# FP4 input groups quantised, scaled and turned in two halves, with the second three slots later, and two slots' exponentials moved up

## What is computed

```python
x = L0_attn_x                                  # (2, 2048, 128)
h = _layernorm(x) * (1 + ca) + sa
x = x + ga * attention(h, Wq, Wk, Wv)          # RoPE, causal up to one key beyond
h = _layernorm(x) * (1 + cb) + sb
x = x + gb * ffn(h)                            # all three products in FP4
...
def fp4_quant_dequant(x):
    xb = x.reshape(shape[:-1] + (shape[-1] // 16, 16))
    scale = jnp.maximum(jnp.max(jnp.abs(xb), axis=-1, keepdims=True) / 6.0, 1e-12)
    xn = xb / scale
    idx = jnp.searchsorted(_MID, jnp.abs(xn))
    return (_GRID[idx] * jnp.sign(xn) * scale).reshape(shape)
def ffn(x):                                    # w_gate, w_up: (352, 128)
    return fp4_linear(silu(fp4_linear(x, w_gate)) * fp4_linear(x, w_up), w_down)
```

## Time and profile before

| what | value |
|---|---|
| median of 3 runs | 661.08 us (659.02 to 661.5) |
| the profiled execution's own time | 660.58 us |
| its span, from first to last instruction | 658.8 us |
| busy: PE, DVE, ACT, POOL | 609.0, 464.8, 355.0, 246.5 us |
| mean granted TensorE clock | 0.994 |

### The profile page before, as it was taken

The page is one execution under the profiler, slowest core; times in us unless marked ns, Lnnn a source line. Parts: engine busy times, 40 slices in busy tenths (PEclk is TensorE's granted clock), DMA queues, the critical chain, the costliest instruction groups (busy, mean ns, idle before and its releaser), DMA issues.

```text
span 658.8 us, 10990 instructions
## 1 busy us (share of the span) xinstructions
PE 609.0 (92%) x3763; PEld 477.3 (72%) x3763; DVE 464.8 (71%) x1265; ACT 355.0 (54%) x740; POOL 246.5 (37%) x305
## 2 busy tenths in 40 slices
PE   7998899989799899999989998888999999999997
PEld 5665777868576777785668787666677888777775
DVE  3887689786787447826668978679756673777765
ACT  4334554665545464453445456555656556666554
POOL 4275655453764321003556545467452100000000
PEclk9998999999899999999999999999999999999999
DMA  8300000000000000000000000020000000000101
GB/s 250 108 1 1 1 1 1 1 0 1 1 1 0 1 1 1 1 1 1 0 1 1 1 1 1 0 61 2 1 1 0 1 1 1 1 1 16 36 29 48
DMA packets 12494, 9.65 MB, mean 15 GB/s; under 512 B 1868, under 2 KB 10904, under 8 KB 12440
## 3 DMA queue, kind: packets, MB, share of 16 engines
q1 hardware_dynamic: 12440, 8.95, 4.6%
HBM read 6.84 MB, written 2.10 MB: 14 GB/s over the span
## 4 chain that ended last, share of the span: by engine, by line
PE 68%; DVE 13%; ACT 9%; POOL 5%; issue 4%; DVEq 0%; ACTq 0%; POOLq 0%
PE ps L1008 14%; PE ps L860 11%; PE ps L986 8%; PE ps L1192 4%; PE ps L1194 4%; PE ps L1193 4%; PE ps L800 4%; ACT xn L1359 2%; PE ps L1034 2%; PE ps L1035 2%; PE ps L1052 2%; POOL rstd L645 2%; DVE row_max L1836 2%; PE ps L795 2%; ACT probs L1399 1%
## 5 line engine op out<-in xcount | busy, mean ns | idle before, releaser
L1425 ACT ACTIVATE probsT<-ps 128x512 f32<-128x512 f32 (+3 forms) x160 | 85.3, 533 | 155.4 <-PE ps L986 155.3
L1008 PE MATMUL ps<-v_sb,probsT 128*128 128x129 f32 (+1 forms) x1124 | 152.0, 279 | 2.6 <-ACT probsT L1427 2.6
L1008 PEld LDWEIGHTS ps<-v_sb,probsT 128*128 128x128 f32 (+1 forms) x1124 | 137.7, 191 | 7.4 <-ACT probsT L1427 4.0
L1836 DVE TENSOR_REDUCE row_max<-ps 128x1 f32<-128x512 f32 (+2 forms) x144 | 87.5, 619 | 54.1 <-PE ps L868 26.7
L986 PE MATMUL ps<-ident,probs 128*128 128x128 f32 (+1 forms) x562 | 90.4, 277 | 16.1 <-ACT hT L1352 7.8
L986 PEld LDWEIGHTS ps<-ident,probs 128*128 128x128 f32 (+1 forms) x562 | 63.4, 139 | 47.8 <-issue 43.3
L1399 ACT ACTIVATE probs<-ps,neg_max 128x512 f32<-128x512 f32 (+7 forms) x158 | 93.0, 620 | 8.6 <-DVE neg_max L1843 8.4
L684 POOL TENSOR_TENSOR hq<-ha,hp 128x352 f32<-128x352 f32 x32 | 29.8, 932 | 100.5 <-DVE hp L1886 100.5
L860 PE MATMUL ps<-k_high,q_high 128*128 128x512 f32 (+5 forms) x100 | 42.0, 420 | 8.2 <-ACT probs L1399 8.2
L644 POOL TENSOR_SCALAR minus_mean<-mv 128x4 f32<-128x4 f32 (+1 forms) x16 | 3.8, 235 | 106.5 <-DVE veps L1586 106.3
L1520 ACT ACTIVATE probs<-ps 128x512 f32<-128x512 f32 x40 | 23.9, 598 | 26.4 <-PE ps L1185 24.2
(11 more groups left out here) (294 smaller groups left out, 1402.5 us busy)
## 6 DMA issues: line engine op xcount, KB each, us to landing
out<-x_sb SPq DMA_DIRECT2D x7, 256.0 KB, 2.3
hT_all<-in_L_wmod SPq DMA_DIRECT2D x2, 384.0 KB, 5.3
x_sb<-in_L_attn_x SPq DMA_DIRECT2D x2, 256.0 KB, 4.7
rope_cos<-table_cos SPq DMA_DIRECT2D x2, 256.0 KB, 4.6
rope_sin<-table_sin SPq DMA_DIRECT2D x2, 256.0 KB, 6.4
x_sb<-in_L_attn_x SPq DMA_DIRECT2D x1, 512.0 KB, 5.8
rope_cos<-table_cos SPq DMA_DIRECT2D x1, 512.0 KB, 6.6
rope_sin<-table_sin SPq DMA_DIRECT2D x1, 512.0 KB, 7.6
```

The lines of the kernel that those rows point to most:

```text
L1008: mm = pe.matmul(bank(OUT_AT, 0, V_W), probsT[0:size, n % 4, k * P:(k + 1) * P], v_sb[0:size, j, :], start=(c == 0 and k == 0), stop=(c == ...
L1425: ins = act.activation(probsT[:, n % 4, 0:full], bank(TURN, 0, full), ACT.Copy)
L1836: ins = dve.tensor_reduce(dst, ps[:, start:start + width], AX.X, ALU.max, negate=single)
```

## The change

`FP4_PARTS` becomes two halves of two tiles. DVE quantises the first half of group g at the end of slot 4g + 4, as before, and the second half in slot 4g + 7, behind the maxima of that slot and ahead of `quantise_h`. POOL's `xq_scaled` of the second half stands in slot 4g + 7, ahead of `hq_scaled`. PE turns the first half at the start of slot 4g + 6 and the second at the start of slot 4g + 8. Group 0 is special: DVE quantises its first half in slot 5, behind the maxima, and PE turns it in slot 6 behind the scores and the projection instead of ahead of them. In slots 4 and 5 ACT takes the exponentials of the next tile at the end of the chunks, which in slot 4 is ahead of `normalise_1` and in both slots ahead of the rounding of rotated groups (`round_rope`, L1453).

```diff
-FP4_PARTS = ((0, 1), (1, GROUP))
+FP4_PARTS = ((0, 2), (2, GROUP))
...
-    firsts = (("fp4_first", FFN_LAG), ("fp4_rest", FFN_LAG + 1), ("norm2", DOWN_LAG + GROUP + 1), ("norm3", TILES + GROUP + 2))
+    firsts = (("fp4_first", FFN_LAG), ("fp4_rest", FFN_LAG + 2), ("norm2", DOWN_LAG + GROUP + 1), ("norm3", TILES + GROUP + 2))
...
+EARLY_EXP_SLOTS = (GROUP, GROUP + 1)
...
+FP4_REST_SLOT = FP4_SLOT + 3
...
+                    if at(FP4_REST_SLOT) is not None:
+                        xq_scaled(at(FP4_REST_SLOT), 1)
                     if ffn_tile(s, FFN_LAG) is not None:
                         hq_scaled(s - FFN_LAG)
...
-                        xq_scaled(at(FP4_SLOT))
+                        xq_scaled(at(FP4_SLOT), 0)
...
                     for key in input_turns(b, s):
-                        turn_group(key)
+                        if key != ("fp4_first", 0):
+                            turn_group(key)
                     if following:
                         scores(s + 1, 0)
                     project_0_in(s)
                     project_1(s)
+                    if s == FFN_LAG:
+                        turn_group(("fp4_first", 0))
...
-                    if s:
+                    if s and s - 1 not in EARLY_EXP_SLOTS:
                         exp(s, 0)
-                    if n > 1:
-                        exp(s, 1)
+                        if n > 1:
+                            exp(s, 1)
...
+                        if s in EARLY_EXP_SLOTS and c == turns - 1:
+                            exp(s + 1, 0)
+                            exp(s + 1, 1)
                         if c == min(1, turns - 1) and group_at(s, NORM1_SLOT + 1) is not None:
                             normalise_1(group_at(s, NORM1_SLOT + 1))
...
-                def fp4_input(g):
+                def fp4_input(g, part):
                     def scales_used():
-                        if g:
+                        if b or g:
                             dve.wait_ge(xq_ready, 2 * (b * GROUPS + g))
...
+                    if s == FP4_SLOT + 1:
+                        fp4_input(0, 0)
+                    if group_at(s, FP4_REST_SLOT) is not None:
+                        fp4_input(group_at(s, FP4_REST_SLOT), 1)
                     normalise_in_slot(s)
...
-                    if group_at(s, FP4_SLOT) is not None:
-                        fp4_input(group_at(s, FP4_SLOT))
+                    if group_at(s, FP4_SLOT):
+                        fp4_input(group_at(s, FP4_SLOT), 0)
```

More of the change, by code:

```diff
@@ L690, in hq_scaled, with xq_scaled @@
                         [P, INNER // BLOCK, BLOCK]), ALU.mult).then_inc(hq_ready, 1)
-                def xq_scaled(g):
-                    pool.wait_ge(xq_grid, b * GROUPS + g + 1)
+                def xq_scaled(g, part):
                     if g >= 1:
                         pool.wait_ge(turned, TURN_AT[b, "fp4_rest", g - 1] + 1)
[L696 to L705, removed]
+                    a, z = FP4_PARTS[part]
+                    cols, done = slice(a * P, z * P), b * 4 * GROUPS + 4 * g + 2 * part
+                    pool.wait_ge(xq_grid, 2 * (b * GROUPS + g) + part + 1)
+                    pool.tensor_tensor(xq[:, cols], qa[:, cols], qp[:, cols], ALU.add).then_inc(xq_step, 1)
+                    pool.wait_ge(xq_step, done + 1)
+                    pool.tensor_tensor(xq[:, cols], xq[:, cols], qp[:, cols], ALU.subtract).then_inc(xq_step, 1)
+                    pool.wait_ge(xq_step, done + 2)
+                    by_block = xq[:, cols].rearrange("p (k e) -> p k e", e=BLOCK)
+                    scales = qs[:, 2, a * P // BLOCK:z * P // BLOCK].unsqueeze(2)
+                    pool.tensor_tensor(by_block, by_block, scales.to_broadcast([P, (z - a) * P // BLOCK, BLOCK]),
+                                       ALU.mult).then_inc(xq_ready, 1)
                 def rope_sum(g, which):
@@ L1016, in gate_up @@
                         pe.wait_ge(weights_ready, 4)
-                    if t < 2:
-                        out_of_bank((("fp4_first", "fp4_rest")[t], g))
+                    if t % 2 == 0:
+                        out_of_bank((("fp4_first", "fp4_rest")[t // 2], g))
                     if n >= 1:
@@ L1887, in quantise @@
                     return last
-                def fp4_input(g):
+                def fp4_input(g, part):
                     def scales_used():
-                        if g:
+                        if b or g:
                             dve.wait_ge(xq_ready, 2 * (b * GROUPS + g))
-                    dve.wait_ge(h_shifted, len(FP4_PARTS) * (b * GROUPS + g + 1))
-                    quantise(qa[:], qp[:], xn[:, g, :], GROUP * P // BLOCK, qs, scales_used).then_inc(xq_grid, 1)
+                    a, z = FP4_PARTS[part]
+                    cols, blocks_at = slice(a * P, z * P), slice(a * P // BLOCK, z * P // BLOCK)
+                    dve.wait_ge(h_shifted, len(FP4_PARTS) * (b * GROUPS + g) + part + 1)
+                    quantise(qa[:, cols], qp[:, cols], xn[:, g, cols], (z - a) * P // BLOCK, qs[:, :, blocks_at],
+                             scales_used).then_inc(xq_grid, 1)
                 def combine(n):
```

## The result

The changed kernel takes 686.81 us (median of 4 runs, 684.4 to 688.98) against 660.41 us before (median of 4, 659.02 to 661.5): 1.040 times as long, 95% interval 1.0352 to 1.0448. The profiled execution took 685.22 us with a span of 683.4 us and a mean granted clock of 0.978; before it was 660.58, 658.8 and 0.994.

What follows compares the result with a forecast made beforehand. PE, busy for 92% of the span, was taken to bound the kernel. Idle time of +8.7 us (batch 1) and +7.8 (batch 0), together +16.5, plus 2.5 for the clock, on 660.6 gave 679.6 us; range 667 to 689.

Steps and rivals of the forecast that it cites:

- the third rival: Each new wait on PE drops the clock: six drops, 10.2 us, giving 687 us; chance 0.12.
- The second halves: PE waits at slots 8, 12 and 20: +2.84, +3.33, +3.62 us in batch 1; +1.65, +3.33, +3.62 in batch 0.
- The chain: From `neg_max` through DVE's and POOL's work on a half to PE's turn: 4.4 us, bounds 4.0 and 4.7.
- Slots 4 to 6: Early exponentials and the later first half of group 0 together lose 1.15 us in each batch.
- What comes back: Idle time before slots 10 and 19 goes: 0.95 and 1.33 us in batch 1, 0.6 and 1.33 in batch 0.
- The sum: Losses less what comes back: +8.7 us in batch 1, +7.8 in batch 0, together +16.5 us.
- The clock: Six new PE waits bring three drops to half clock, 5.1 us, of which 2.5 us were taken.
- Half of it comes back: Rival: the waits come, but other engines get ahead and later waits shrink; 670 us, chance 0.22.
- The price of a half: Quantising one FP4 half takes DVE 2.0 us, between 1.63 and 2.27; POOL's share is 2.2 us.
- The first rival: Second halves hide behind other work and the kernel gets faster by about 10.5 us, to 650; chance 0.06.

Runs made afterwards that it cites:

- the halves placed group by group: Changed kernel without early exponentials or special group 0; second halves in slot 4g+6 (groups 0, 1), 4g+7 (group 2), behind the first half (group 3): 660.44 us.

## Why the prediction was right, and where it was not

The time, 686.81 us, lies in the range of 667 to 689 and 7 us above the predicted 679.6. It lies above the forecast's own bounds, 673 to 685, too: the range holds it because it took in the start of the third rival. So the mechanism was right, and that the time fell inside the range is partly luck. Step by step:

- **The second halves** came as forecast, and are most of the loss. Forecast and measured idle time ahead of the turns: slot 8, 2.84 and 2.83 us (batch 0: 1.65 on top of 0.79, measured 2.50); slot 12, 3.33 and 3.20; slot 16, nothing and nothing; slot 20, 3.62 and 3.70. The chain was put at 4.4 us and is 4.5. The run with the half a slot earlier shows that the place is the cause: 19.6 us come back.
- **Slots 4 to 6**: forecast a loss of 1.15 us up to `gate_up` of tile 0; measured, from `neg_max` of tile 0, 0.92 us in batch 1 (352.80 less 306.67 against 340.70 less 295.49) and 1.0 in batch 0. Two waits of 1.9 us were forecast; in batch 1 1.60 and 1.67 were measured, in batch 0 1.97 and 0.36. Two details were wrong. In batch 0 a wait of 1.40 us stays before the scores of tile 6, because `neg_max` of tile 5 is itself later there; I had taken batch 1 for both. And the 0.57 us that PE waits for the copy of `xqT` were within my allowance for ACT's copies, not named as a wait. That the early exponentials are a loss, and by 1.0 us per batch ahead of any half clock, the runs on them alone show.
- **What comes back**: in slot 10 0.4 and 0.5 us instead of 0.6 and 0.95. In slot 19 the wait is gone in batch 1, as forecast, but in batch 0 it was only 0.68 us and 0.18 of it stays, and in batch 1 the turn of group 3's first half in slot 18 now waits 0.48 us. These terms were too large by 1.9 us together (4.2 forecast, 0.39 + 0.54 + 0.50 + 1.33 - 0.48 measured).
- **The sum** of these was +16.5 us of idle time; measured are +17.8.
- **The clock** is the term that was mis-sized: three drops, discounted to 2.5 us, were forecast. There are 30.7 us at 0.50 instead of 6.8, PE's busy time grew by 6.8 us, and filling the six waits gave back 9.1 us. Five of the six waits were followed by half clock (once from within the wait on, and twice as long), not half of them. So the time is that of the third rival (each wait drops the clock, 687), which had 0.12; without the half clock behind the waits the kernel measures 677.7, where the sum without its clock term says 677.1 (10.2 us at 0.50 are left in that run, where the kernel before has 6.8). The Trainium skill, page "TensorE: Matmul & The Clock Gate", section "Part 1: The HAM clock gate", has half rate as the default that activity lifts. That 9 us came back when throwaway matmuls kept PE busy agrees with it; that the wait of 3.20 us in batch 1 was followed by full clock and the equal one of batch 0 by half agrees with its schedule of its own.
- **Half of it comes back** was wrong: from slot 20 on nothing does, PE is 13.5 us behind in batch 1 (the ends of `neg_max` of tiles 0 and 31 are 251.75 us apart before and 265.25 after) and stays so.
- **The price of a half** on DVE, 2.0 us, holds where POOL is idle, as in slots 7, 11 and 19. The forecast had no term for POOL at work beside it, and the first halves needed one: at the ends of slots 8 and 16 of batch 0 they take 2.73 and 3.60 us, with POOL's `hq_scaled` beside them, where the whole group took 3.26 and 3.62 before. So DVE is relieved there by 0.5 us and by nothing instead of 1.25, which fits what came back in slots 10 and 18, and DVE's busy time grew by 11.2 us (464.8 to 476.0), not by about 6. The division alone costs 11.6 us with both halves in the old place, so in a kernel with other places the forecast would have been wrong.
- **The first rival's sum** is a slip: its terms as listed, twice 5.33 us and a drop of 1.7, make 12.4 us and 648, not 10.5 and 650. No chance hangs on it.

What stays open is how the 7 us that remain between the earlier second half (667.2) and the kernel before divide exactly: without the early exponentials 3 to 4 of them go, and another 2.8 us went in the run with the halves placed group by group, which changed groups 0, 2 and 3 at once and does not separate them.

## What to carry to other kernels

When a producer is divided so that its second part starts later, write down the whole chain from its new start to its consumer, every engine in it, and set it against the consumer's start in each place: here 4.5 us stood against 0.8 to 1.6, and it could be read from the trace before. A wait on PE costs its length and the half clock that may follow it, here about 1.5 us for each of the six waits (9.1 us); price both. Before you move independent work in front of a waiting instruction, see whether that work already covers the hand-back of the buffer behind it: here that took back what the move gained. And before you divide DVE's work, see whether the engine that it feeds would be at work beside the second part: here that made two halves of 5.7 us out of a whole of 3.26.

## What the runs showed of the hardware

DVE's instructions of 256 columns took 0.42 us (`qa`) and 0.29 us (`qp`, from `qa`) with POOL idle, and in the run of the division alone 0.73 and 0.77, 0.59 and 0.76 us where an instruction of POOL overlapped them; the halves of 2.0 us took 2.8 and 3.0 us there. In that run's lines above, each `qa` ended 0.28 or 0.29 us behind the end of the POOL instruction that was running (372.19 behind 371.90, 375.27 behind 374.99), and each of these `qp` 0.14 us behind (372.98 behind 372.84, 375.89 behind 375.75). The TENSOR_REDUCE of `qs` took 0.40 us beside POOL (370.49) and 0.41 without it (364.57). The Trainium skill, page "SBUF — State Buffer", section "SBUF: two separate sides", says that DVE and GpSimd share one pair of ports, which is a lock held for a whole instruction, not a split of bandwidth: a DVE instruction in a two-port mode, or with two inputs in SBUF while GpSimd reads SBUF, can wait there for one of GpSimd. The ends above agree: these DVE instructions end just behind POOL's.

Waits of 1.6 and 2.0 us (60.07 before, 65.95 after) were followed by half clock, and one of 3.20 us (409.06) was not.
